# Attention in phases of two key tiles, with maxima over two PSUM banks and the row sums split over transfers, GpSimd and a few matmuls with ones

## The reference

```python
h = _ada_ln(x, cond, Wln1, bln1)
q, k, v = heads(h @ Wq + bq), heads(h @ Wk + bk), heads(h @ Wv + bv)
scores = jnp.einsum('bhqd,bhkd->bhqk', q, k) / np.sqrt(HD)
attn = jax.nn.softmax(scores, axis=-1)
out = jnp.einsum('bhqk,bhkd->bhqd', attn, v)
x = x + out.transpose(0, 2, 1, 3).reshape(B, L, D) @ Wo + bo
h = _ada_ln(x, cond, Wln2, bln2)
x = x + jax.nn.gelu(h @ W1 + b1, approximate=False) @ W2 + b2
# then: graph attention over the first 20 nodes, twice, and v + relu(...)
```

## Time and profile before

| | |
|---|---|
| median of three runs | 3489.25 us (3487.66 to 3492.49) |
| the profiled execution | 3488.01 us |
| its span, first to last instruction | 3486.7 us |
| TensorE busy | 3386.5 us, 97% |
| VectorE busy | 2146.7 us, 62% |
| GpSimd busy | 1782.1 us, 51% |
| ScalarE busy | 1463.1 us, 42% |
| transfers | 222.77 MB, 64 GB/s over the span |

### The profile page before, as it was taken

How to read it: one execution, slowest core, us unless ns; L and a number is a source line. 1 busy time by engine, 2 the same in 40 slices (tenths; PEclk the granted TensorE clock), 3 DMA queues, 4 the chain that set the end, 5 groups by cost and what they waited for, 6 DMA issues and landing times.

```text
span 3486.7 us, 49344 instructions
## 1 busy us (share of the span) xinstructions
PE 3386.5 (97%) x18874; PEld 2231.8 (64%) x18874; DVE 2146.7 (62%) x3650; ACT 1463.1 (42%) x2803; POOL 1782.1 (51%) x836
## 2 busy tenths in 40 slices
PE   8789999999999999999999996999999999999999
PEld 7677655555555555555555542778888888778888
DVE  4648677777777777777777787743333333226666
ACT  2111366666666666666666665311111111112322
POOL 0200599898898989889898975410000000002222
PEclk9999999999999999999999999999999999989999
DMA  5463400303003030030210000831111110301221
GB/s 197 139 205 130 131 19 11 80 19 71 19 10 80 10 80 20 10 80 10 64 26 19 22 13 26 299 117 37 37 37 37 37 37 27 109 32 61 70 71 57
DMA packets 140498, 222.77 MB, mean 64 GB/s; under 512 B 14148, under 2 KB 56380, under 8 KB 137191
## 3 DMA queue, kind: packets, MB, share of 16 engines
q1 hardware_dynamic: 140263, 219.62, 21.6%
HBM read 143.55 MB, written 75.50 MB: 63 GB/s over the span
## 4 chain that ended last, share of the span: by engine, by line
PE 91%; DVE 4%; DMA 2%; issue 1%; ACT 1%; POOL 1%; SPq 0%; DVEq 0%; ACTq 0%; POOLq 0%
PE ps L337 17%; PE ps L632 14%; PE ps L620 13%; PE ps L1120 10%; PE ps L1109 10%; PE ps L639 4%; PE ps L432 4%; PE ps L1640 3%; PE ps L1653 2%; PE ps L982 2%; PE ps L436 2%; DVE pacc L802 2%; PE ps L1673 2%; PE ps L1470 1%; PE ps L151 1%
## 5 line engine op out<-in xcount | busy, mean ns | idle before, releaser
L362 DVE TENSOR_REDUCE nmp<-ps 128x1 f32<-128x512 f32 x2048 | 1278.9, 683 | 411.2 <-PE ps L337 410.6
L726 ACT ACTIVATE pt<-ps 128x512 f32<-128x512 f32 x2048 | 1080.9, 601 | 611.0 <-PE ps L620 597.5
L821 POOL TENSOR_TENSOR pacc<-pacc,pt 128x1024 f32<-128x1024 f32 x420 | 1000.6, 2382 | 116.2 <-ACT pt L726 90.0
L337 PE MATMUL ps<-ks,qs 96*128 96x512 f32 x2048 | 865.9, 430 | 17.6 <-DVE nmp L362 17.0
L620 PE MATMUL ps<-qs,ks 128*128 128x512 f32 x2048 | 818.7, 404 | 14.2 <-ACT pt L726 10.7
L337 PEld LDWEIGHTS ps<-ks,qs 96*128 96x128 f32 x2048 | 379.8, 189 | 413.9 <-DVE nmp L362 265.0
L632 PE MATMUL ps<-pt,vq 128*32 128x512 f32 x4096 | 547.5, 607 | 0.0
L620 PEld LDWEIGHTS ps<-qs,ks 128*128 128x128 f32 x2048 | 389.0, 191 | 104.5 <-ACT pt L726 42.1
L829 POOL TENSOR_TENSOR paccb<-paccb,pt 128x1024 f32<-128x1024 f32 x172 | 424.4, 2468 | 10.0 <-ACT pt L726 7.7
L1120 PE MATMUL ps<-w,gp 128*128 128x512 f32 x1536 | 381.5, 397 | 3.8 <-DVE gp L1253 3.8
L1109 PE MATMUL ps<-hpb,w 128*128 128x512 f32 x1536 | 380.4, 397 | 3.4 <-DMA x_d<-x 3.4
(11 more groups left out here) (172 smaller groups left out, 3256.5 us busy)
## 6 DMA issues: line engine op xcount, KB each, us to landing
qk_d<-st SPq DMA_DIRECT2D x128, 256.0 KB, 2.7
ks<-qk_d SPq DMA_DIRECT2D x24, 1024.0 KB, 12.5
qs<-qk_d SPq DMA_DIRECT2D x96, 256.0 KB, 5.3
xina<-in_x SPq DMA_DIRECT2D x8, 1024.0 KB, 6.3
v_d<-vst SPq DMA_DIRECT2D x32, 256.0 KB, 2.4
vq<-v_d SPq DMA_DIRECT2D x8, 1024.0 KB, 18.5
ao_d<-aop SPq DMA_DIRECT2D x8, 1024.0 KB, 5.3
ao<-ao_d SPq DMA_DIRECT2D x32, 256.0 KB, 4.3
```

The source lines that it names most:

```text
L337: pe.matmul(ps[:, cnt.bank["max", u], :], qsb[0:96, v % 4, hh, 128 * qt:128 * qt + 128], ksb[w % 2][0:96, hh, CH * kc:CH * kc + CH], start ...
L362: dve.tensor_reduce(nmp[:, hq, kc:kc + 1], ps[:, cnt.bank["max", u], :], AX.X, ALU.max, negate=True).then_inc(s_mr, 1)
L726: act.activation(pt[:, g % 4, half, c0:c0 + CH], ps[:, (n + 1) % 3, :], ACT.Exp, scale=SCALE).then_inc(s_exp, 1)
L821: pool.tensor_tensor(pacc[:, v % 2, :], pt[:, (g - 1) % 4, 0, :] if kt == 1 else pacc[:, v % 2, :], pt[:, g % 4, 0, :], ALU.add).then_inc( ...
```

## The change

It rewrites the attention on all engines and takes one step out of the output stage.

- **Phases.** The loops run over p, 256 phases of two key tiles, eight a unit (f counts them in it). A phase has eight scores and eight matmuls of maxima in the order `ORDER` (s a score, m a maximum), and then the values of the two tiles of the phase before, one after the other. Scores keep three banks (0 to 2); the values now collect in bank 7.
- **Maxima over two banks.** Two matmuls of maxima write two neighbouring banks, and VectorE reduces both with one instruction into two columns. There are two such pairs of banks (3 and 4, 5 and 6), used in turn, also by the row's turn (before phase 6's matmuls) and the sums (after those of phase 0). `pe_pair_free` waits for the use before the last. In the projections 84 steps are done instead of 108, one bank at a time as before. There are no extra maxima.
- **Row sums.** pt is eight tiles deep. GpSimd issues a transfer for each odd tile but the last, which copies (tiles 1 and 3) or adds (5 to 13) all four heads' pt, 1 MB, to one of two accumulators accd. It adds the even tiles, 128 x 2048 at a time, to pacc. Tile 15, both accd and pacc go through ones once a unit (`pe_sums`), 512 columns each, all in one bank, after phase 0 of the next unit.
- **Output feature by query.** Nothing is turned. VectorE copies the sums out of PSUM (phase 1), SP folds the four rows of sums to 128 partitions by 16 (rs), VectorE inverts them (after phase 2), SP stores them in r_d and loads them repeated over 32 partitions each (recb, phase 3), and VectorE multiplies accv and recb (after phase 4). SP stores the product after each unit, in ao_d, which holds features by queries per tile.
- **Output stage.** `pe_out_turn` is gone. ScalarE and VectorE read the loaded tile from SBUF.
- **Smaller things.** Queries have three buffers instead of four, loaded two units ahead. accv and accs are single. The keys' first buffer and the layer norm's weights lie at the top of SBUF. Wo is loaded in unit 28, and its parts are split in unit 30 as before.

The core of the diff (removed lines stand in the listing above; blank lines are left out):

```diff
+EARLY = 84
+ADD_DMA = (1, 3, 5, 7, 9, 11, 13)
+ADD_POOL = (0, 2, 4, 6, 8, 10, 12, 14)
+ADD_PE = (15,)
+ORDER = ("s", "m", "m", "s", "m", "s", "m", "s", "s", "m", "s", "m", "s", "m", "m", "s")
...
+        for p in range(NGRP // 2):
+            v, f = divmod(p, 8)
+            if f == 6 and v + 1 < NU:
+                self.use(("row", v + 1))
+            for i in range(4):
+                if EARLY // 2 - 1 + 4 * p + i < 32 * NU:
+                    self.use(("max", EARLY // 2 - 1 + 4 * p + i))
+            if f == 0 and v:
                 self.use(("sums", v - 1))
...
-        pt = take("pt", [128, 4, 2, 2 * CH])
-        pacc = take("pacc", [128, 2, 2 * CH])
-        paccb = take("paccb", [128, 2 * CH])
-        accv = take("accv", [128, 2, CH])
-        accs = take("accs", [128, 2, CH])
+        pt = take("pt", [128, 8, 4, CH])
+        accd = take("accd", [128, 2, 4, CH])
+        pacc = take("pacc", [128, 4, CH])
+        accv = take("accv", [128, CH])
+        accs = take("accs", [128, CH])
+        recb = take("recb", [128, CH])
+        aout = take("aout", [128, 2, CH])
         ones = take("ones", [128, 32])
-        aop = take("aop", [128, 2, S // 128, 128])
         rs = take("rs", [128, 16])
-        wtmpo = take("wtmpo", [128, NK, D])
-        wo = place("wo", [128, 2, NK, D], nc.sbuf_top - 16384, F32R)
+        rr = take("rr", [128, 16])
...
+        def pe_pair_free(what):
+            if ring.before[what] is None:
+                return
+            kind, n = ring.before[what]
+            if kind == "max":
+                pe.wait_ge(s_mr, max_count(n // 32, 2 * (n % 32) + 1))
+            elif kind == "row":
+                pe.wait_ge(s_nh, 2 * n + 2)
+            else:
+                pe.wait_ge(s_accs, n + 1)
+        def pe_max(p, half):
+            v, n = p // 32, 2 * (p % 32) + half
+            w = v // NCH
+            hq, kc = divmod(n, 4)
+            if n == 0:
+                pe.wait_ge(s_qd[v % 3], 48 * (v // 3 + 1))
+                pe.wait_ge(s_kd[w % 2], 48 * (w // 2 + 1))
+            if half == 0:
+                pe_pair_free(("max", p))
+            m = pe.matmul(ps[:, ring.bank["max", p] + half, :], qsb[0:96, v % 3, hq // 4, 128 * (hq % 4):128 * (hq % 4) + 128],
+                          ksb[w % 2][0:96, hq // 4, CH * kc:CH * kc + CH], start=True, stop=True)
+            if half:
+                m.then_inc(s_mm, 1)
+        def pe_row(v):
+            pe.wait_ge(s_nm, v + 1)
+            pe_pair_free(("row", v))
+            pe.transpose(ps[0:16, ring.bank["row", v], 0:128], nm[:, :], ident[:, :]).then_inc(s_nt, 1)
...
+        def dve_max(p):
+            v, n = p // 32, 2 * (p % 32)
+            bank = ring.bank["max", p]
+            if n == 0:
+                dve.wait_ge(s_nm, v)
+            dve.wait_ge(s_mm, max_count(v, n))
+            dve.tensor_reduce(nmp[:, n // 4, n % 4:n % 4 + 2], ps[:, bank:bank + 2, :], AX.X, ALU.max,
+                              negate=True).then_inc(s_mr, 1)
...
+                m = pe.matmul(ps[32 * hh:32 * hh + 32, 7, :], vq[:, w % 2, kt, 32 * hh:32 * hh + 32],
+                              pt[:, g % 8, hh, :], start=(kt == 0), stop=(kt == 15))
...
+        def pe_ones(bank, src, start, stop):
+            for hh in range(4):
+                m = pe.matmul(ps[32 * hh:32 * hh + 32, bank, :], ones[:, :], src[:, hh, :], start=start, stop=stop)
+            return m
+        def pe_sums(v):
+            bank = ring.bank["sums", v]
+            pe_pair_free(("sums", v))
+            for kt in ADD_PE:
+                pe_ones(bank, pt[:, (16 * v + kt) % 8, :, :], kt == ADD_PE[0], False)
+            for i in range(2):
+                pe.wait_ge(s_dma[i], dma_count(v, ADD_DMA[len(ADD_DMA) - 1 - (len(ADD_DMA) - 1 - i) % 2]))
+                pe_ones(bank, accd[:, i, :, :], False, False)
+            pe.wait_ge(s_add, add_count(v, ADD_POOL[-1]))
+            pe_ones(bank, pacc[:, :, :], False, True).then_inc(s_end, 1)
 
...
+            for p in range(NGRP // 2):
+                v, f = divmod(p, 8)
+                if f == 6 and v + 1 < NU:
+                    pe_row(v + 1)
+                ns = nm_ = 0
+                for what in ORDER:
+                    if what == "s":
+                        pe_scores(2 * p + ns // 4, ns % 4)
+                        ns += 1
                     else:
+                        pair = EARLY // 2 - 1 + 4 * p + nm_ // 2
+                        if pair < 32 * NU:
+                            pe_max(pair, nm_ % 2)
+                        nm_ += 1
+                if p:
+                    pe_values(2 * p - 2)
+                    pe_values(2 * p - 1)
+                if f == 0 and v:
+                    pe_sums(v - 1)
+            pe_values(NGRP - 2)
+            pe_values(NGRP - 1)
+            pe_sums(NU - 1)
...
+            if g >= 8 and hh == 0:
+                ev, ekt = divmod(g - 8, 16)
+                act.wait_ge(s_pv, g - 7)
+                if ekt in ADD_DMA:
+                    act.wait_ge(s_dma[ADD_DMA.index(ekt) % 2], dma_count(ev, ekt))
+                elif ekt in ADD_POOL:
+                    act.wait_ge(s_add, add_count(ev, ekt))
                 else:
+                    act.wait_ge(s_end, ev + 1)
+            act.activation(pt[:, g % 8, hh, :], ps[:, n % 3, :], ACT.Exp, scale=SCALE).then_inc(s_exp, 1)
+        def act_values(v):
+            act.wait_ge(s_pv, 16 * v + 16)
+            if v:
+                act.wait_ge(s_an, v)
+            act.activation(accv[:, :], ps[:, 7, :], ACT.Copy).then_inc(s_accv, 1)
...
+        def dve_sums(v):
+            dve.wait_ge(s_end, v + 1)
             if v:
+                dve.wait_ge(s_rsd, 16 * v)
+            dve.tensor_copy(accs[:, :], ps[:, ring.bank["sums", v], :]).then_inc(s_accs, 1)
+        def dve_recip(v):
+            dve.wait_ge(s_rsd, 16 * (v + 1))
+            if v:
+                dve.wait_ge(s_rw, 16 * v)
+            dve.reciprocal(rr[:, :], rs[:, :]).then_inc(s_rec, 1)
+        def dve_values(v):
+            dve.wait_ge(s_recb, 16 * (v + 1))
+            dve.wait_ge(s_accv, v + 1)
+            if v >= 2:
+                dve.wait_ge(s_ao[v % 2], 16 * (v // 2))
+            dve.tensor_tensor(aout[:, v % 2, :], accv[:, :], recb[:, :], ALU.mult).then_inc(s_an, 1)
...
+                if f == 6 and v + 1 < NU:
+                    dve_row_split(v + 1, ring.bank["row", v + 1])
+                if f == 1 and v:
+                    dve_sums(v - 1)
+                for i in range(4):
+                    pair = EARLY // 2 - 1 + 4 * p + i
+                    if pair < 32 * NU:
+                        dve_max(pair)
+                        if pair % 32 == 31:
+                            dve_row_max(pair // 32)
+                if f == 2 and v:
+                    dve_recip(v - 1)
+                if f == 4 and v:
+                    dve_values(v - 1)
...
+                if kt in ADD_DMA:
+                    j = ADD_DMA.index(kt)
                     pool.wait_ge(s_exp, 4 * g + 4)
+                    if j >= 2:
+                        pool.wait_ge(s_dma[j % 2], dma_count(v, kt) - 16)
+                        pool.dma_start(accd[:, j % 2, :, :], pt[:, g % 8, :, :], accum_op=ALU.add).then_inc(s_dma[j % 2], 16)
+                    else:
+                        if v:
+                            pool.wait_ge(s_end, v)
+                        pool.dma_start(accd[:, j % 2, :, :], pt[:, g % 8, :, :]).then_inc(s_dma[j % 2], 16)
+                elif kt in ADD_POOL[1:]:
+                    pool.wait_ge(s_exp, 4 * g + 4)
+                    if kt == ADD_POOL[1]:
+                        if v:
+                            pool.wait_ge(s_end, v)
+                        first = pt[:, (16 * v + ADD_POOL[0]) % 8, :, :]
+                    else:
+                        pool.wait_ge(s_add, add_count(v, kt) - 1)
+                        first = pacc[:, :, :]
+                    pool.tensor_tensor(pacc[:, :, :], first, pt[:, g % 8, :, :], ALU.add).then_inc(s_add, 1)
...
+        def sp_fold_sums(v):
+            sp.wait_ge(s_accs, v + 1)
+            if v:
+                sp.wait_ge(s_rec, v)
+            sp.dma_start(rs[:, :], accs[0:128:32, :].rearrange("h (c i) -> h c i", i=16)).then_inc(s_rsd, 16)
+        def sp_store_recip(v):
+            sp.wait_ge(s_rec, v + 1)
+            if v >= 2:
+                sp.wait_ge(s_recb, 16 * (v - 1))
+            sp.dma_start(r_d[v % 2].rearrange("h (c i) -> (h c) i", i=16), rr[:, :]).then_inc(s_rw, 16)
+        def sp_load_recip(v):
+            sp.wait_ge(s_rw, 16 * (v + 1))
+            if v:
+                sp.wait_ge(s_an, v)
+            sp.dma_start(recb[:, :], r_d[v % 2].unsqueeze(1).to_broadcast([4, 32, CH])).then_inc(s_recb, 16)
         def sp_store_ao(v):
+            w, qc = divmod(v, NCH)
+            b, k = divmod(w, 4)
+            t0 = 16 * b + 4 * qc
+            sp.wait_ge(s_an, v + 1)
```

(26 more changed lines are left out.)

472 lines of the change are left out of this document (126 added, 346 removed).

## The result

The changed kernel takes 3507.5 us (median of 20 runs, 3490.4 to 3515.1) where the kernel before took 3491.1 beside it (20 runs): ratio 1.0046, 95% interval 1.0034 to 1.0057, a little slower and surely so. The forecast was 3435. The profiled execution is the lowest of those runs, 3490.4 us.

The account below looks back on a forecast made before the run. TensorE's instructions and what they wait for were taken as the bound. 3488.0 - 5.6 (earlier start) - 47.6 (first to last score) + 4.5 (tail) - 5 (output stage) = 3434.3, given as 3435 for the median; range 3345 to 3630.

Parts of the forecast that it names:

- The chain that folds, inverts and broadcasts the sums: Between a unit's sums and VectorE's product: four phases are available for some 10 us of work, so no cost.
- the queues passed: SP's queue in the attention: SP waits there in order, but row copy and query loads have 12 us and more.
- Rival (2): Accumulating transfers set the attention's pace: a loss from a landing of 11.8 us, 3627 us at three streams; chance 0.18.
- rival (3): GpSimd becomes the attention's bound through its transfer issues: no gain at 2.0 us each, 3705 us at 3; chance 0.16.
- First to last score: Attention from first to last score, with phases, ones, row turns and held products: 1716.7 us against 1764.3, 47.6 less.
- Earlier start: Attention's start: 24 maxima fewer in the projections, at 0.235 us each, bring the first score 5.6 us earlier.
- Tail: From last score to output stage: late sums, small transfers, product and store take 22.5 us against 17.2; net +4.5.
- Output stage: Losing 32 turns saves 5 us, between 0 and 10, since transfers limit it and VectorE may be held.
- The phase: Two key tiles in the attention: 5.81 us without stalls, 6.18 with 0.37 of waits for the two pairs of banks.
- The product held by GpSimd: VectorE's scaling after phase 4's maxima waits for GpSimd's add of SBUF data, lengthening phase 5 by 0.95 us a unit.
- Rival (1): Full gain in the attention: quick enough reduction and no held product, 120 us less, 3316 us; chance 0.17.
- Rival (4): TensorE's saved mode entries return one for one as waits for the two pairs of banks: 3489 us; chance 0.07.

Follow-up runs that it names:

- e9: Changed kernel with each maximum taken over 256 of a bank's 512 keys, leaving half the keys out of the maxima: 3452.0 us, 0.9904.
- e4: Changed kernel with VectorE's product of values and inverted sums two units after its sums, where GpSimd is idle: 3459.0 us, 0.9917.
- e5: On e4, the reciprocal and its store moved to phase 4, the broadcast's load behind the row copy in phase 6: 3462.4 us, 0.9925.
- e10: On e4, reciprocal after phase 3, broadcast in phase 5 before the row copy, group loads one at a time in phase 1 or 6: 3443.0 us.
- e3: Changed kernel with transfers into the sums moving 16 columns, the plain copies from the second unit on; odd tiles leave the row sums: 3416.8 us.
- e11: On e4, reciprocal and store in phase 4, broadcast in phase 5, one group load per unit in phase 2: 3392.7 us, 0.9717.

## Why the prediction was wrong

**The failed step** is "The chain that folds, inverts and broadcasts the sums has four phases for some 10 us", costed at nothing, with the line on the queues passed ("its row copy (phase 6) and query loads have 12 us and more"). Both took landings like those of the earlier trace rows, from a kernel whose attention keeps the transfer engines at 0.16, for one at 0.75, and passed over the group's own loads, which landed in 12.5 and 18.5 us even there. In the long units the chain takes some 34 us of transfers, which makes six units 75.4 us too long; in the first unit the row copy comes 13 us late, the larger part of 21. Rival (2) had noted that 1 MB is asked for every 6.2 us, but used it only for the accumulating transfers themselves. Behind the first unit they keep their deadline; the small ones beside them lose theirs. The 0.34 on slower stood on rivals (2) and (3), and neither came: the kernel lost by what no rival named.

**The sum, term by term** (profiled execution, 3434.3 forecast, 3490.4 measured):

- First to last score: 1798.2 (373.1 to 2171.3) against 1716.7, +81.5: six long units 75.4, the first unit about 21 (76.9, where nine phases of 6.17 would be 55.5), less 31 x 0.48 for ordinary units of 53.62 instead of 54.1.
- Earlier start: 18.0 (373.1 against 391.1) instead of 5.6, -12.4. 24 maxima fewer in the projections were priced on TensorE alone. Part of the rest is chance: in the fourteen runs behind it, whose projections are the same, the first score comes at 375.6 to 383.7, later than here. With their median, 377.7, some 8 us stay unexplained.
- Tail: 29.1 from the last score to the first output matmul against 25.8, +3.3 for a forecast of +4.5. Output stage: -2.6 for -5.
- Everything behind it: 14.2 less, in stages that the change leaves alone. The runs' median is 17 above this execution, so I count none of it as a gain. Without it the terms add up to 70.3, and between the medians the miss is 72 (3507.5 against 3435.5).

**What held.** The phase: 6.17 from one pair of values to the next (chain below), 6.18 forecast; values of two tiles 1.85 for 0.99 + 0.86; the reduction 1.219 us for 1.22, with its stall (e9). The product held by GpSimd: 0.77 a unit (e4) for 0.95. The add 4.59 for 4.6, an issue 0.87 or 0.61 where I took 1.3, so rival (3) had nothing to it. The accumulating transfer landed in 8.8 us (L780), a plain copy of the same size in 4.7 (L784), where I took 9.2 and 5.2. By the half rate that the Trainium skill gives an adding transfer (Collectives: The Full Stack, § The bandwidth ceiling: the fold count and why AG ≠ RS ≠ AR), the trace agrees. TensorE waits for one at the ones only once, at the very end, so rival (2) did not come, though e5 and e10 show how near it is. Rival (1), that neither stall would be there, fell: e4 and e9 each gained by taking one away. Rival (4) did not come either, since ordinary units are 1.8 us shorter than before. Without the transfers' load e3 gives 3417, close to what the forecast's units promised.

```profile
664.99 1.85 PE ps L643 x16
...
671.16 1.85 PE ps L643 x16
```

## What to carry to other kernels

Moving work from an engine to transfers is priced in the time of the sixteen engines (here 4.6 us for each megabyte, the mean of five added and two copied), summed with all other traffic of the busiest unit, not of the mean: at 0.7 an 8 KB store landed in 1.4 us, in a unit that began at 1.03 the same store took 8.9 and the gathering before it 18. A chain of small dependent transfers then needs its allowance as much as the large ones. Spread the bulk loads and place each where nothing with a near deadline lies behind it: by e4's and e11's moves together, with no work taken away, the changed kernel went from 0.5% slower than before to 2.8% faster.

## What had not been expected of the hardware

- An 8 KB transfer took 18.3 us behind 3 MB of loads beside accumulating ones, 15 from another engine's queue, and as long in 32 or 16 rows as in 128.
- The mean share does not decide: over the attention e11 is at 0.81 with ordinary units of 52.8 to 53.0 throughout, the changed kernel at 0.75 with six long ones, each with 27 us at 1.03 to 1.05 in it.
- In a stretch of 13 us without TensorE's work the granted clock was 0.72, and in the next 9 us 0.65; ordinary units run at 1.00, the level of 2.4 GHz (the others are means over it and 1.2 GHz).
